# Expert projections of a transformer's last layer: one fp32 product each, or three bf16 products in pairs of experts

## The chip, the cores and the metric

The kernel is one program on one core of a Trainium2 chip. A core has five engines that run their own instruction lists side by side: TensorE (PE in the profile; PEld is its weight load), VectorE (DVE), ScalarE (ACT), GpSimd (POOL) and SyncE (SP), which here only issues DMAs. They meet at semaphores. Matmul results land in PSUM, in eight banks of 128 partitions x 512 fp32 words; GpSimd works on SBUF alone in this kernel. The metric is device microseconds (us) of one execution.

## What is computed

The reference is a stack of four blocks, each a gated cross attention and a gated feed-forward part, on 4 batches x 512 tokens x 128 features. The change is in the last part, a mixture with 16 experts of head dimension 64. Its core:

```python
rw = _gating(hidden_states, sim_matrix, gates)            # (4, 512, 16), softmax over active experts
q = einsum('bte,bted->btd', rw, einsum('btc,ecd->bted', hidden_states, q_proj))
k = einsum('bte,bted->btd', rw, einsum('btc,ecd->bted', hidden_states, k_proj))
v = einsum('bte,bted->btd', rw, einsum('btc,ecd->bted', hidden_states, v_proj))
scores = einsum('bqd,bkd->bqk', q, k) / 8                 # then causal mask
attn = einsum('bqk,bkd->bqd', softmax(scores), v)
mixed = attn[:, :, None, :] * rw[..., None]
return einsum('bted,edc->btc', mixed, o_proj)
```

So q, k and v are each a sum over 16 experts of (token scaled by its expert weight) times the expert's matrix. Everything is fp32 in the reference.

## The kernel before

The kernel runs eight stages one behind the other (numbers 0 to 7 in its names); every engine has one method per stage and its order is the order of the Python code. No scheduler moves anything. The stage that changes is the last, `mixture_*`.

Its order of work is set by `mixture_steps`. Per batch b it yields the steps x = 0 to 15, one per expert, and then the closing step x = 16. Beside the experts of batch b, the steps carry the pieces of attention and output of batch b-1: steps 0 to 5 its softmax attention in four query tiles (`scores`, then `turn` = transpose of the probabilities, then `weigh` = product with v), steps 6 to 14 its output, in 8 pairs of experts (`scale` = spread the pair's weights over partitions, `bring` = product with `o`). After the last batch the pieces of batch 3 run alone.

What one expert needs:
- TensorE, L2464 (`weights_of`): a bf16 selector product that spreads the expert's row of token weights over 128 partitions, in one of four rotating PSUM banks.
- VectorE, L2624: this times the transposed tokens `xt`, written as fp32 to `scaled7`, of which there are four buffers.
- TensorE, `products`, two steps later: L2472, `qk` weights (128 columns) times `scaled7` into bank 4, and L2476, `v` weights (64 columns) into partitions 0 to 63 of bank 5 for even experts and 64 to 127 for odd ones. Both are fp32 with 512 moving columns; the trace shows each such matmul as two records.

At the closing step ScalarE copies bank 4 in two halves (L2547, L2548) and bank 5 (L2551), TensorE adds the two halves of v with four small products (L2489), and VectorE copies the result (L2630). In the attention steps, one tile of scores passes through a chain: TensorE L2498 and the mask L2499, VectorE maximum L2636 and its scaling L2637, ScalarE exponential L2559, VectorE reciprocal L2640 and normalising L2641, TensorE transposes L2504, ScalarE copy L2565, TensorE `weigh` L2512. The output uses TensorE L2464 again (`scale`), VectorE L2648, TensorE L2524 (`bring`).

GpSimd has nothing to do after the router at the start of the stage (L2661, L2662). Splitting fp32 words into a high and a low bf16 half is already done in other stages: `halves` views a word as two bf16 numbers, of which number 1 is the high half of the word, and a subtraction writes (word - high half) over the low half. `products` at L472 then makes three bf16 products (high x high, high x low, low x high). L952 is such a subtraction, on GpSimd, in stage 0, and L708 multiplies its results there with 64-column weights. `onehead_po` is GpSimd's part of stage 2; L415 is the power that every layer normalisation needs.

## Time and profile before

| | us |
|---|---|
| median of 3 runs | 2001.94 (2001.07 to 2005.05) |
| the profiled execution: its own time | 2000.12 |
| the profiled execution: span from first to last instruction | 1998.3 |
| TensorE busy | 1573.0 (79%) |
| VectorE busy | 1167.4 (58%) |
| ScalarE busy | 801.3 (40%) |
| GpSimd busy | 644.1 (32%) |

A busy TensorE is not one at its peak, since its records overlap; how long a matmul holds the engine is read from the distance between starts. The profile also gives the clock that TensorE was granted, as a share of full speed: 1.00 is 2.4 GHz and 0.50 is 1.2 GHz. Times in the trace count from the start of the span.

### The profile page before, as it was taken

The page shows a single profiled execution, that of the slowest core. Times are in us where ns is not written, and L with a number is a line of the kernel's source. Part 1 is how long each engine was busy: PE and PEld are TensorE (multiplying, and loading weights), DVE is VectorE, ACT ScalarE, POOL GpSimd, SP SyncE. Part 2 cuts the span into 40 slices and gives each one's busy share as a digit, 9 for nine tenths or more (in the row PEclk, how much of TensorE's full clock was granted, in tenths as well). Part 3 has the DMA queues.
Part 4 walks back from the last instruction along what each step waited for, and adds up shares of the span by engine and source line. Part 5 has one row for each costly group of instructions (what it writes and reads, how often), then busy time and mean ns, then how long its engine had stood idle before and what let it go on. Part 6 is the DMA issues. An engine that isn't in the chain of part 4 may idle for free.

```text
span 1998.3 us, 31337 instructions
## 1 busy us (share of the span) xinstructions
PE 1573.0 (79%) x11217; PEld 993.7 (50%) x11325; DVE 1167.4 (58%) x2856; ACT 801.3 (40%) x1803; POOL 644.1 (32%) x770
## 2 busy tenths in 40 slices
PE   4899889988998986675268789959957867399997
PEld 2566656666666665553155345524442334224444
DVE  4766676666666654546947656554574566633333
ACT  3666556746655663420034245533213432100011
POOL 3677567756654862500012333000003101100000
PEclk9999989999998997866568799989985788599987
DMA  6223211201111212310000000000000000000000
GB/s 241 67 82 103 71 53 40 52 22 43 48 37 37 55 32 69 103 75 0 0 1 1 10 4 1 2 0 1 1 0 1 1 1 1 0 0 6 6 1 11
DMA packets 35439, 63.89 MB, mean 32 GB/s; under 512 B 7527, under 2 KB 25026, under 8 KB 34131
## 3 DMA queue, kind: packets, MB, share of 16 engines
q1 hardware_dynamic: 33815, 59.77, 10.0%
q0 software_dynamic: 1472, 2.12, 0.3%
q8 instruction: 93, 1.52, 0.3%
q14 instruction: 59, 0.48, 0.1%
HBM read 30.59 MB, written 12.66 MB: 22 GB/s over the span
## 4 chain that ended last, share of the span: by engine, by line
PE 53%; DVE 24%; issue 6%; ACT 5%; DMA 4%; POOL 4%; SPq 2%; ACTq 0%; DVEq 0%; POOLq 0%
PE banks L475 9%; PE banks L693 4%; PE banks L1860 3%; DVE work L738 3%; PE banks L2476 3%; PE banks L682 3%; PE banks L708 3%; PE banks L2472 3%; DVE xn L421 3%; DMA work<-scratch 3%; SPq L987 2%; PE banks L1843 2%; PE banks L634 2%; PE banks L450 2%; PE banks L2524 1%
## 5 line engine op out<-in xcount | busy, mean ns | idle before, releaser
L952 POOL TENSOR_TENSOR work<-work 128x512 bf16<-128x512 f32 (+1 forms) x448 | 373.2, 861 | 59.5 <-ACT work L850 57.6
L835 ACT ACTIVATE work<-banks,work 128x666 f32<-128x666 f32 x256 | 209.1, 817 | 250.5 <-DVE work L738 185.3
L738 DVE TENSOR_REDUCE work<-banks 128x1 f32<-128x666 f32 x256 | 215.8, 843 | 66.8 <-PE banks L682 66.2
L693 PE MATMUL banks<-const,work 128*128 128x128 f32 (+1 forms) x1536 | 229.3, 281 | 22.7 <-ACT work L850 19.3
L415 POOL TENSOR_TENSOR norm_room<-norm_room,minus_half 128x4 f32<-128x4 f32 x48 | 50.1, 1045 | 562.8 <-DVE norm_room L410 562.8
L682 PE MATMUL banks<-work 128*128 128x154 bf16 (+1 forms) x935 | 171.2, 302 | 27.6 <-DMA work<-scratch 21.6
L693 PEld LDWEIGHTS banks<-const,work 128*128 128x128 f32 (+1 forms) x1536 | 156.1, 135 | 54.1 <-issue 20.3
L708 PE MATMUL banks<-work 128*64 128x256 bf16 x2304 | 159.4, 283 | 15.3 <-POOL work L952 14.2
L475 PE MATMUL banks<-work,weights_b 128*128 128x512 bf16 (+1 forms) x830 | 157.2, 347 | 13.2 <-DVE work L2184 5.6
L450 PE MATMUL banks<-const,xn 128*128 128x128 f32 x176 | 40.9, 375 | 142.3 <-DVE xn L421 89.4
L850 ACT ACTIVATE work<-banks 128x512 f32<-128x512 f32 x256 | 151.0, 590 | 3.9 <-PE banks L693 3.8
L682 PEld LDWEIGHTS banks<-work 128*128 128x128 bf16 x1024 | 96.6, 99 | 110.0 <-DMA work<-scratch 28.7
L756 DVE COPY work<-banks 128x256 f32<-128x256 f32 x256 | 106.0, 414 | 63.3 <-PE banks L693 63.1
L708 PEld LDWEIGHTS banks<-work 128*64 128x64 bf16 x2304 | 120.9, 110 | 34.9 <-POOL work L952 17.4
L1937 DVE TENSOR_REDUCE work<-banks 128x2 f32<-128x308 f32 x192 | 86.5, 472 | 83.1 <-PE banks L1815 45.2
L456 ACT ACTIVATE xt<-banks 128x512 f32<-128x512 f32 x48 | 28.5, 597 | 247.4 <-PE banks L450 247.2
L475 PEld LDWEIGHTS banks<-work,weights_b 128*128 128x128 bf16 (+1 forms) x840 | 82.9, 100 | 83.6 <-issue 18.4
L1916 ACT ACTIVATE work<-banks 128x256 f32<-128x256 f32 (+1 forms) x256 | 87.3, 382 | 61.5 <-PE banks L1847 26.9
L450 PEld LDWEIGHTS banks<-const,xn 128*128 128x128 f32 x176 | 26.8, 188 | 154.6 <-DVE xn L421 72.7
L1843 PE MATMUL banks<-work 128*128 128x256 bf16 (+1 forms) x256 | 66.9, 293 | 14.4 <-ACT work L1908 11.6
L750 DVE TENSOR_TENSOR work<-banks,work 128x256 f32<-128x256 f32 x64 | 27.2, 424 | 86.6 <-ACT work L844 86.6
L931 POOL COPY work<-work 128x256 f32<-128x256 f32 x64 | 25.4, 397 | 144.4 <-DVE work L746 144.4
(386 smaller groups left out, 3047.8 us busy)
## 6 DMA issues: line engine op xcount, KB each, us to landing
work<-work SPq DMA_DIRECT2D x128, 166.5 KB, 2.9
sorted<-in_pads SPq DMA_DIRECT2D x10, 838.5 KB
weights_b<-in_weights SPq DMA_DIRECT2D x1, 4120.0 KB, 25.0
work<-scratch SPq DMA_DIRECT2D x64, 64.0 KB, 2.4
weights_b<-in_weights SPq DMA_DIRECT2D x1, 2824.0 KB, 9.8
weights_a<-in_weights SPq DMA_DIRECT2D x1, 2056.0 KB, 8.6
weights_a<-in_weights SPq DMA_DIRECT2D x1, 2050.0 KB, 10.4
work<-work SPq DMA_DIRECT2D x32, 64.0 KB, 1.9
```

Source lines behind the costliest of these rows:

```text
L450: i = pe.transpose(ps[:, j * P:j * P + rows], src[0:rows, j, :], self.eye[0:rows, 0:rows])
L475: m = pe.matmul(out, left(a), right(b), start=start and n == 0, stop=stop and n == 2)
L682: m = pe.matmul(slot[:, a:z], lhs, k[:, h, part, a:z], start=part == 0, stop=part == 1)
L693: m = pe.transpose(ps[0:rows, c:c + P], prob[:, t * P:t * P + rows], self.eye)
L708: m = pe.matmul(self.out_bank[64 * h:64 * h + 64, 0:2 * P], self.v[n % 3][:, t, of_values, 64 * h:64 * h + 64], self.probs_parts[u % 2][:, ...
L738: ve.tensor_reduce(self.neg_max[i % 4], self.slot[i % 2][:, 0:KEYS0], AX_X, ALU.max, negate=True).then_inc(self.mark("max"))
L756: ve.tensor_copy(self.probs_t[u % 2][:, h, 4:KT0, j * P:(j + 1) * P], self.bank_b[:, 0:2 * P].rearrange("p (t n) -> p t n", t=2)).then_inc ...
L835: ac.activation(self.probs[i % 3], self.slot[i % 2][:, 0:KEYS0], ACT.Exp, bias=self.neg_max[i % 4], accum_out=self.sums[u % 2][:, 2 * j + ...
L850: ac.activation(self.probs_t[u % 2][:, h, 0:4, j * P:(j + 1) * P], self.bank_a.rearrange("p (t n) -> p t n", t=4), ACT.Copy).then_inc(self ...
L952: po.tensor_tensor(parts[:, :, :, 0], exact, parts[:, :, :, 1], ALU.subtract).then_inc(self.mark(event, i - 3))
L1843: m = pe.matmul(bank, left, a.q4[b % 2][:, g, cols], start=True, stop=s != 4)
L1916: ac.activation(out, self.bank_of(k, HALF)[0:rows_n, :], ACT.Exp).then_inc(self.mark("exp4", s, n))
```

## The change

Three edits.

1. The fp32 products of `products` become three bf16 products each, made for two experts at a time. The six `qk` products are issued first (L475, from the helper), then six `v` products with even and odd expert alternating. `products` is now called at the odd steps 3, 5, ..., 15 for the pair (x-3, x-2) and at the closing step for the pair (14, 15). Its semaphore counts pairs. `scaled7` has six buffers in place of four.
2. GpSimd makes the low halves of `scaled7`: one subtraction of 128 x 512 per expert and batch, 64 in all, each behind VectorE's multiplication; the products wait for it (`scaled7_low`).
3. GpSimd makes the low halves of the `qk` and `v` weights once, in stage 2: six subtractions of 128 x 512, behind a wait for the weights' DMA.

```diff
     def onehead_po(self, po):
         self.follow_power(po, 1, BATCH - 1)
+        po.wait_ge(*self.at("dma_weights7", 16))
+        for name in ("qk", "v"):
+            for c in range(self.w[7][name].shape[1] // BANK):
+                whole = self.w[7][name][:, c * BANK:(c + 1) * BANK]
+                po.tensor_tensor(self.halves(whole)[:, :, 0], whole, self.halves(whole)[:, :, 1], ALU.subtract).then_inc(self.mark("low7"))
...
-        self.scaled7 = [self.place(SEQ) for _ in range(4)]
+        self.scaled7 = [self.place(SEQ) for _ in range(6)]
...
         def products(b, x):
-            n = E3 * b + x
-            z = self.scaled7[n % 4]
+
+            both = (x, x + 1)
+            words = {e: self.halves(self.scaled7[(E3 * b + e) % 6]) for e in both}
             if x == 0:
                 self.bank(pe, 4, "projected7_k", b)
-            pe.wait_ge(*self.at("scaled7", n))
-            pe.matmul(self.bank_of(4), w["qk"][:, x * P:(x + 1) * P], z, start=x == 0, stop=x == E3 - 1)
-            if x == 0:
                 self.bank(pe, 5, "projected7_v", b)
-            o = slice(64 * (x % 2), 64 * (x % 2) + 64)
-            pe.matmul(self.bank_of(5)[o, :], w["v"][:, x * D3:(x + 1) * D3], z, start=x < 2, stop=x >= E3 - 2).then_inc(self.mark("products7", n))
+            for e in both:
+                pe.wait_ge(*self.at("scaled7_low", E3 * b + e))
+                of = self.halves(w["qk"][:, e * P:(e + 1) * P])
+                self.products(pe, self.bank_of(4), lambda part: of[:, :, 1 - part], lambda part: words[e][:, :, 1 - part], e == 0, e == E3 - 1)
+            for n, (of, at) in enumerate(((1, 1), (1, 0), (0, 1))):
+                for e in both:
+                    o = slice(64 * (e % 2), 64 * (e % 2) + 64)
+                    m = pe.matmul(self.bank_of(5)[o, :], self.halves(w["v"][:, e * D3:(e + 1) * D3])[:, :, of], words[e][:, :, at],
+                                  start=e < 2 and n == 0, stop=e >= E3 - 2 and n == 2)
+            m.then_inc(self.mark("products7", E3 // 2 * b + x // 2))
...
                 weights_of(spread1[0:96, x, :], b, "scaled7", E3 * b + x).then_inc(self.mark("spread_weights7", E3 * b + x))
-                if x >= 2:
-                    products(b, x - 2)
+                if x >= 3 and x % 2:
+                    products(b, x - 3)
             elif x == E3:
                 products(b, E3 - 2)
-                products(b, E3 - 1)
...
                 ve.wait_ge(*self.at("spread_weights7", n))
-                if n >= 4:
-                    ve.wait_ge(*self.at("products7", n - 4))
+                if n >= 6:
+                    ve.wait_ge(*self.at("products7", (n - 6) // 2))
...
         po.memset(self.parts7[0:96, :], 0.0).then_inc(self.mark("clear7"))
+        po.wait_ge(*self.at("clear7", 1))
+        for n in range(BATCH * E3):
+            po.wait_ge(*self.at("scaled7", n))
+            z = self.scaled7[n % 6]
+            po.tensor_tensor(self.halves(z)[:, :, 0], z, self.halves(z)[:, :, 1], ALU.subtract).then_inc(self.mark("scaled7_low", n))
```

Where the instructions stand. First TensorE in batch 0, in the middle of the experts; before, one selector product (L2464) and one expert (L2472, L2476) alternate, with the semaphore that each waits for in brackets:

```order
L2464 MATMUL banks<-work,const_b 128x512 [waits scaled]
L2472 MATMUL banks<-work,weights_a 128x512 [waits scaled]
L2476 MATMUL banks<-work,weights_a 64x512
L2464 MATMUL banks<-work,const_b 128x512 [waits scaled]
L2472 MATMUL banks<-work,weights_a 128x512 [waits scaled]
L2476 MATMUL banks<-work,weights_a 64x512
```

and now (L2470 is the selector, L475 the `qk` products, L2486 the `v` products):

```order
L2470 MATMUL banks<-work,const_b 128x512 [waits scaled] x2
L475 MATMUL banks<-work,weights_a 128x512 [waits scaled_low]
L475 MATMUL banks<-work,weights_a 128x512 x2
L475 MATMUL banks<-work,weights_a 128x512 [waits scaled_low]
L475 MATMUL banks<-work,weights_a 128x512 x2
L2486 MATMUL banks<-work,weights_a 64x512 x6
```

Two selectors now stand together, and a pair's twelve products behind them; the wait of the products is for GpSimd's result in place of VectorE's.

Second, TensorE in a later batch, from step 2 to step 5, where the attention of the batch before runs. Before (L2504 is `turn`, L2498 and L2499 `scores`, L2512 `weigh`):

```order
L2464 MATMUL banks<-work,const_b 128x512
L2472 MATMUL banks<-work,weights_a 128x512
L2476 MATMUL banks<-work,weights_a 64x512
L2504 MATMUL banks<-const,work 128x128 x2
L2498 MATMUL banks<-work 128x256
L2498 MATMUL banks<-work 128x128
L2499 MATMUL banks<-const_b 128x128
L2512 MATMUL banks<-work 128x128
L2464 MATMUL banks<-work,const_b 128x512
L2472 MATMUL banks<-work,weights_a 128x512
L2476 MATMUL banks<-work,weights_a 64x512
L2504 MATMUL banks<-const,work 128x128 x3
```

and now (L2515 is `turn`, L2509 and L2510 `scores`, L2523 `weigh`):

```order
L2470 MATMUL banks<-work,const_b 128x512
L2515 MATMUL banks<-const,work 128x128 x2
L2509 MATMUL banks<-work 128x256
L2509 MATMUL banks<-work 128x128
L2510 MATMUL banks<-const_b 128x128
L2523 MATMUL banks<-work 128x128
L2470 MATMUL banks<-work,const_b 128x512
L475 MATMUL banks<-work,weights_a 128x512 x6
L2486 MATMUL banks<-work,weights_a 64x512 x6
L2515 MATMUL banks<-const,work 128x128 x3
```

The products of step 2 have gone from between the selector and the transposes; those of a pair stand in step 3. Step 4 loses its products in the same way and step 5 has the next pair.

Third, the end of GpSimd's list, which ended with the memset before:

```order
-L2661 TENSOR_TENSOR work<-work,half 128x16
-L2662 MEMSET work 96x2048
-L2726 UNCONDITIONAL_BRANCH
+L2671 TENSOR_TENSOR work<-work,half 128x16
+L2672 MEMSET work 96x2048
+L2677 TENSOR_TENSOR work<-work 128x512 x64
+L2741 UNCONDITIONAL_BRANCH
```

The 64 new subtractions (L2677) run in GpSimd's list behind everything it had.

## Rows read from the trace of the kernel before

In a timeline a row is start (us), length (us), engine, line, operation, operands, count, and in brackets how long the engine had been idle and what ended it.

**Rows 1.** each batch's end at L2547 (start us, us, what, [idle before])
```profile
1785.19 0.59 ACT L2547 ACTIVATE work<-banks 64x512 f32<-64x512 f32 x1 [46.45 <-PE banks L2476]
...
1841.70 0.59 ACT L2547 ACTIVATE work<-banks 64x512 f32<-64x512 f32 x1 [34.24 <-PE banks L2476]
...
1900.05 0.59 ACT L2547 ACTIVATE work<-banks 64x512 f32<-64x512 f32 x1 [34.24 <-PE banks L2476]
...
1959.98 0.59 ACT L2547 ACTIVATE work<-banks 64x512 f32<-64x512 f32 x1 [34.24 <-PE banks L2476]
```

**Rows 2.** critical chain of the stretch 1747 to 1960 us, shares by line
```profile
by line: PE banks L2476 31.0%; PE banks L2472 27.9%; PE banks L2464 11.5%; PE banks L2524 10.3%; PE banks L2498 4.8%; PE banks L2512 3.6%; PE banks L2504 2.8%; PE banks L2489 1.7%; issue 1.4%; DVE work L2624 1.3%; DVE work L2611 1.1%; PE ba
```

**Rows 3.** timeline of the stretch 1756 to 1763 us, one expert of batch 0
```profile
1756.94 0.39 PE L2464 MATMUL banks<-work,const_b 96*128 96x512 bf16 x1
...
1757.17 1.02 PE L2472 MATMUL banks<-work,weights_a 128*128 128x512 f32 x2
...
1757.37 0.69 DVE L2624 TENSOR_TENSOR work<-banks,xt 128x512 f32<-128x512 f32 x1 [1.49 <-PE banks L2464]
...
1758.12 1.07 PE L2476 MATMUL banks<-work,weights_a 128*64 128x512 f32 x2
...
1759.13 0.39 PE L2464 MATMUL banks<-work,const_b 96*128 96x512 bf16 x1
```

**Rows 4.** timeline of ScalarE in stage 5, each start behind 12 bf16 products
```profile
1380.17 0.69 ACT L2174 ACTIVATE work<-banks,weights_b 128x512 f32<-128x512 f32 x1 [1.90 <-PE banks L475]
...
1382.76 0.69 ACT L2174 ACTIVATE work<-banks,weights_b 128x512 f32<-128x512 f32 x1 [1.90 <-PE banks L475]
```

**Rows 5.** timeline of TensorE in stage 1, moving halves of words, 256 columns
```profile
795.70 2.95 PE L475 MATMUL banks<-work,weights_b 128*128 128x256 bf16 x24
...
798.49 0.38 PE L1172 MATMUL banks<-const,work 128*128 128x128 f32 x2
```

**Rows 6.** timeline of TensorE in stage 0, the 64-column products of L708
```profile
401.23 0.73 PE L682 MATMUL banks<-work 128*128 128x512 bf16 x4
...
401.89 1.22 PE L708 MATMUL banks<-work 128*64 128x256 bf16 x18
...
403.04 0.33 PE L693 MATMUL banks<-const,work 128*128 128x128 f32 x1
```

**Rows 7.** instruction groups of GpSimd (xcount | busy us, mean ns | idle before)
```profile
L952 POOL TENSOR_TENSOR work<-work 128x512 bf16<-128x512 f32 x256 | 267.2, 1044 | 59.5 <-ACT work L850 57.6
```

**Rows 8.** timeline of GpSimd in stage 2
```profile
852.63 1.01 POOL L415 TENSOR_TENSOR norm_room<-norm_room,minus_half 128x4 f32<-128x4 f32 x1 [3.68 <-DVE norm_room L410]
...
881.44 1.01 POOL L415 TENSOR_TENSOR norm_room<-norm_room,minus_half 128x4 f32<-128x4 f32 x1 [27.80 <-DVE norm_room L410]
```

**Rows 9.** timeline of batch 1, step 2: scores of tile 1 to their transposes
```profile
1792.02 0.23 PE L2499 MATMUL banks<-const_b 128*128 128x128 bf16 x1
...
1792.83 0.69 DVE L2624 TENSOR_TENSOR work<-banks,xt 128x512 f32<-128x512 f32 x1
...
1793.73 0.35 DVE L2641 TENSOR_SCALAR work<-work 128x256 f32<-128x256 f32 x1
...
1794.27 0.44 PE L2504 MATMUL banks<-const,work 128*128 128x128 f32 x2
```

**Rows 10.** normalising scalings of VectorE, first in stage 0, then behind it
```profile
L421 DVE TENSOR_SCALAR xn<-x,norm_room 128x128 f32<-128x128 f32 x12 | 7.2, 660 | 0.0
...
L421 DVE TENSOR_SCALAR xn<-xn,norm_room 128x128 f32<-128x128 f32 x80 | 23.9, 361 | 5.9 <-POOL norm_room L415 5.6
```

**Rows 11.** timeline of both engines at the router's memset
```profile
1719.51 1.80 POOL L2662 MEMSET work<- 96x2048 bf16 x1
...
1719.60 1.74 DVE L2578 TENSOR_SCALAR work<-work 128x16 f32<-128x16 f32 x1 [5.99 <-POOL work L2661]
```

**Rows 12.** windows: length, busy PE, PEld, DVE, ACT, POOL, then TensorE's clock
```profile
1852.00:1854.00 2.00, 2.00 (x10) 1.05 (x9) 0.00 (x0) 0.38 (x1) 0.00 (x0) 1.00 0.00 0
...
1910.00:1912.00 2.00, 2.00 (x3) 0.29 (x2) 0.01 (x1) 0.00 (x0) 0.00 (x0) 0.50 0.00 0
```

More of the change, by code:

```diff
@@ L2459, in mixture_pe @@
         pe.wait_ge(*self.at("parts7", 1))
+        pe.wait_ge(*self.at("low7", 6))
         self.small_at = {}
@@ L2542, in mixture_ac @@
             if x == E3:
-                n = E3 * b + E3 - 1
-                ac.wait_ge(*self.at("products7", n))
+                ac.wait_ge(*self.at("products7", E3 // 2 * (b + 1) - 1))
                 if b >= 2:
@@ L2621, in mixture_ve @@
                 ve.wait_ge(*self.at("spread_weights7", n))
-                if n >= 4:
-                    ve.wait_ge(*self.at("products7", n - 4))
-                ve.tensor_tensor(self.scaled7[n % 4], self.bank_of(self.small_at["scaled7", n]), self.xt[:, self.cols_of(b)],
+                if n >= 6:
+                    ve.wait_ge(*self.at("products7", (n - 6) // 2))
+                ve.tensor_tensor(self.scaled7[n % 6], self.bank_of(self.small_at["scaled7", n]), self.xt[:, self.cols_of(b)],
                                  ALU.mult).then_inc(self.mark("scaled7", n))
```

## The prediction

> **What bounds the kernel now.** I read the chain of waits of the last stage first: from 1747 to 1960 us it stands almost wholly on TensorE, L2476 (`v`) with 31.0% and L2472 (`qk`) with 27.9%, the selector L2464 with 11.5% [rows 2]. So this stretch of 213 us is a TensorE stretch, and the changed instructions are its largest part. Next the ends of the four batches [rows 1]: the experts of batch 0 end at 1785.2, those of batches 1, 2 and 3 after another 56.5, 58.35 and 59.9 us; the 38 us behind 1960 (attention and output of batch 3) hold no changed product. Then the timeline of one expert of batch 0 [rows 3]: selector to `qk` 0.23 us, `qk` to `v` 0.95, `v` to the next selector 1.01. One expert is 2.18 us, its products 1.95, a pair's 3.9. Last I looked at who else is in the loop: VectorE needs 0.43 us from the selector's start and then 0.69 [rows 3]; GpSimd is idle there.
>
> **TensorE's new price.** Six `qk` products per pair: in stage 5, twelve bf16 products of 128x512 pass in 2.59 us [rows 4], 0.216 each, so 1.30. That the moving side is one half of each fp32 word costs nothing: 24 products of that kind with 256 columns pass in 2.79 us, 0.116 each, a little over half of 0.216 [rows 5]. Six `v` products of 64 columns, even and odd expert in different halves of the array: in stage 0, 18 such products with 256 columns take 1.15 us [rows 6], 0.128 for two, so two run side by side. For 512 columns two together lie between 0.216 (one stream) and 0.256 (twice 0.128); I take 0.235, and 0.70 for three. For entering and leaving the 64-column form I add 0.1: the four L682 products ahead, two with 512 and two with 154 columns, should take 0.56 by the 0.216 and take 0.66 [rows 6]. Sum: 2.1 us per pair, bounds 1.95 and 2.7 (no overlap of the `v` products: 1.30 + 6 x 0.216 + 0.1). Saved 1.8 per pair, 32 pairs: 57.6 us.
>
> The Trainium skill, TensorEngine Tiling (Array Packing), Key Properties, says that a change of tiling mode drains TensorE. The 0.1 above is what the row leaves for it; without any drain the 32 pairs would save 3 us more.
>
> **The new link through GpSimd.** One subtraction of 128x512 takes 1.044 us, mean of 256 of the same form, also in place [rows 7]. Two per pair are 2.1, less than the 2 x 0.23 + 2.1 = 2.56 that a pair of batch 0 takes on TensorE. Latency: from the first selector of a pair 0.43 + 0.69 + 0.1 + 1.04 = 2.3 us until the first low half and 3.3 until the second. Between that selector and the pair's products stand the second selector, the products of the pair ahead and two more selectors: 0.23 + 2.1 + 0.46 = 2.8, and 0.65 more until the odd expert is needed, 3.4. So batch 0 is covered, barely; later batches have the attention or output between and are covered well. In the closing step no selectors stand between, some 0.3 us in each batch. The start of batch 0 waits about a us more than before for the first low halves, but at the half clock it starts with; I leave these small ones against each other.
>
> **Where the products were a cover.** In the attention steps, products hid the softmax chain. In batch 1 the mask of tile 1's scores starts at 1792.02 and VectorE's scaling L2641 runs at 1793.73 for 0.35; the transposes start at 1794.27, just when the 1.95 us of products are over [rows 9]. In the new order steps 2 and 4 have no products; those of a pair stand in steps 3 and 5. So in two steps of each of batches 1 to 3 TensorE waits about 1.9 us: 6 x 1.9 = 11.4 us given back. Steps 3 and 5 stay covered. In the output steps nothing was hidden by products that isn't by `bring` (0.9 us).
>
> **A collision of GpSimd and VectorE.** In stage 0, where GpSimd works much, VectorE's scaling of 128x128 takes 0.66 us on average; later 0.36 [rows 10]. At the router a scaling of 128x16 lasts 1.74 us, from 1719.60 to 1721.34, beside GpSimd's memset from 1719.51 to 1721.31 [rows 11]: it came free with it. L2641 is such a scaling and stands in the softmax chain. Its place is bad: the multiplication L2624 ends at 1793.52, GpSimd would start on the low half at about 1793.6 and end at 1794.65, and L2641, due from 1793.73 to 1794.08, would end near 1794.7 [rows 9, 7, 11]. That is 0.6 us for each of four tiles, 12 tiles: 7.2 us lost; bounds 0 and 12 x 1.04 = 12.5.
>
> The Trainium skill, SBUF — State Buffer, Who interferes with whom, says the same: VectorE's two-port forms (scaling and copy within SBUF) and GpSimd take one port pair in turn, the later one blocks wholly. It also says that an operation with one input in PSUM, as L2624, is not hit; without this rule's effect the sum would be 7 us better.
>
> **The clock.** In batch 2 and 3 TensorE falls to 0.50 of its clock after the wait at the batch's end and the first attention steps, and is back at 1.00 at 1852 in the one case and still at 0.50 at 1910 to 1912 in the other [rows 12]. With the same instructions, batches 2 and 3 are 1.85 and 3.4 us longer than batch 1 [rows 1]: that is the price of a fall, 5.2 in all. The new order has more idle time in just these steps (2.5 us in steps 2 and 4, with the collision). I count a fall as in batch 3 in each batch (3.3), and in every second one another in step 4 (2.2): 3 x 4.4 = 13.2, so 8.0 more than now. Bounds: 5.2 less than now (no fall), and half clock through all attention steps, about 8 per batch.
>
> **GpSimd in stage 2.** Six subtractions are 6.3 us. After its power at 852.63 GpSimd is idle until 881.44 [rows 8], so they are hidden; if the weights' DMA were late, 22 us of slack remain. VectorE could be held for one operation there, 1 us at most; I count nothing.
>
> **Sum.** 57.6 - 11.4 - 7.2 - 8.0 = 31.0 us. The profiled execution had 2000.12 (span 1998.3 and 1.8 around it) and would have 1969.1; the median of the runs is 1.8 above it, so 1971.
>
> **Rivals.**
> A. The chain hides better: the clock falls no more often than now, and L2641 slips in ahead of GpSimd. Then 57.6 - 11.4 = 46 us come through, 1956. For it: batch 1 had two waits of 2 us and no fall; against it: the row at 1793.73, behind GpSimd's start.
> B. The `v` products do not overlap at 512 columns: 0.6 per pair, 32 pairs, 19 us: 1990. For it: no row with this width; against it: the 18 products of stage 0, of the same form [rows 6].
> C. GpSimd becomes the bound of batch 0: if its subtraction with waits takes 1.75 us instead of 1.04, a pair needs 3.5 for 2.56: 8 x 0.95 = 8 us, 1979. Against it: 1.044 over 256 instances with small spread, and output steps of 4.8 us per pair that would hide it anyway.
> D. Slower: TensorE does not get its clock back. All from 1747 to 1960 at 0.50: batch 0 then needs 8 x 5.1 = 41 for 38 us, an output phase of 24.3 us (35.1 now less 6 x 1.8) 48.6, the attention phase about 27 for 18.5, with 3 of boundary 79 per batch: 276 for 213, so 2063. Since a us of work at half clock costs half a us, it decides from about 80 us at half clock beyond today's. Against it: a pair's products are over 4 us of unbroken work at half clock, as ahead of the rises [rows 12], and the output steps leave no gap.
> E. The change doesn't do what it says: the wait on the low halves stalls each pair by the 1.8 it saves. It would need a latency of 5.2 in place of 3.3 in batch 0 and more elsewhere: 2000.
>
> **How the numbers follow.** Forecast 52%, own range 1963 to 1980 (the bounds of collision and clock). A 20%, B 9%, C 11%, D 4%, E 2%, and 2% for anything else slower. The predicted time is the forecast's, 1971. For 8 in 10 the range takes in most of A and C: 1955 to 1984. A measurement can tell 0.2% (4 us) from no change. Faster: forecast, A, B, C and the like, 0.94; slower: D and the else, 0.04; the same: E, 0.02.
>
> **What would show it.** Starts of the closing copy: batch 0 should end near 1770.7 instead of 1785.2, the later batches should take 52 to 53 each (56.5 - 14.4 + 3.8 + 2.4 + 4.4); below 49 speaks for A, above 56 for B or D. The twelve products of a pair should take 2.1 us at full clock (2.7: B). TensorE should idle about 2.5 us before the transposes in steps 2 and 4, ended by L2651, the new number of L2641, and this scaling should last over 0.8 us; if it lasts 0.35 the collision is wrong. GpSimd's subtraction should be 1.04 and never the releaser of a long wait. The sum is wrong if products wait long for `scaled7_low` or if any stage ahead of 1700 us changes by over 2 us.

## The result and the profile after

| | before | after |
|---|---|---|
| median of the runs | 2001.81 (4 runs, 2001.07 to 2005.05) | 1973.09 (4 runs, 1971.97 to 1974.64) |
| span of the profiled execution | 1998.3 | 1971.3 |
| stage 7, start to end | 251.18 | 223.99 |
| TensorE busy | 1573.0 | 1535.3 |
| GpSimd busy | 644.1 | 716.6 |

The ratio is 0.9854, with a 95% interval of 0.9837 to 0.9871. The change makes the kernel 28.7 us faster where 31.0 was predicted; 1973 lies 2 us above the forecast and inside its own range. All of the gain is in stage 7: it starts at 1747.31 us where it started at 1747.12. On the way there the two are not level: GpSimd's power (L415) that runs at 991.70 us in before runs at 994.76 in after, though the two were almost level at 852 (852.63 and 852.37), and the difference is gone again by 1100 us. The prediction had named over 2 us ahead of 1700 as a sign against its sum; the two stretches cancel, and the first 2 us of it stand in e10 below as well, which has no new subtractions.

The stage is counted here from the end of VectorE's last router operation to the end of the span. A batch ends at its first closing copy, as in [rows 1]; in ScalarE's timeline of after:

```profile
1772.11 0.59 ACT L2557 ACTIVATE work<-banks 64x512 f32<-64x512 f32 x1 [33.18 <-PE banks L2486]
1827.08 0.59 ACT L2557 ACTIVATE work<-banks 64x512 f32<-64x512 f32 x1 [24.04 <-PE banks L2486]
1879.26 0.59 ACT L2557 ACTIVATE work<-banks 64x512 f32<-64x512 f32 x1 [24.00 <-PE banks L2486]
1932.97 0.59 ACT L2557 ACTIVATE work<-banks 64x512 f32<-64x512 f32 x1 [24.00 <-PE banks L2486]
```

Against [rows 1]: batch 0 takes 24.80 us (38.07 before), the next three 54.97, 52.18 and 53.71 (56.51, 58.35, 59.93), the tail behind them 38.33 (38.32). The forecast was about 23.5 and 52 to 53. ScalarE's idle time ahead of the copy, which is the output stretch without attention, fell from 34.24 to 24.0 in each later batch. The rest of those batches, the attention part, grew from 22.3, 24.1 and 25.7 us to 30.9, 28.2 and 29.7.

The timeline of one pair in batch 0 gives the new price on TensorE:

```profile
1756.24 0.60 PE L2470 MATMUL banks<-work,const_b 96*128 96x512 bf16 x2
...
1756.69 1.52 PE L475 MATMUL banks<-work,weights_a 128*128 128x512 bf16 x6
...
1758.14 0.87 PE L2486 MATMUL banks<-work,weights_a 128*64 128x512 bf16 x6
...
1758.94 0.60 PE L2470 MATMUL banks<-work,const_b 96*128 96x512 bf16 x2
```

From the first `qk` product to the first `v` product 1.45 us, `v` to the next selector 0.80, together 2.25 (2.1 predicted). The whole pair with its two selectors is 2.70 where two experts were 4.37 (2.19 for one [rows 3]), 1.67 less; batch 0 as a whole, with its start, is shorter by 1.66 for each of its eight pairs.

What was given back stands in TensorE's row of the transposes, over the whole stage (busy us, mean ns, then the idle time ahead and who ended it), in after:

```profile
L2515 PE MATMUL banks<-const,work 128*128 128x128 f32 x40 | 10.2, 369 | 28.5 <-DVE work L2651 28.5
```

and in before, whose line is L2504:

```profile
L2504 PE MATMUL banks<-const,work 128*128 128x128 f32 x40 | 9.4, 340 | 11.5 <-DVE work L2641 11.4
```

Both have the same 40 transposes and the same tail. TensorE waits 17.1 us longer for the normalising scaling; the prediction had 18.6 (11.4 for the lost cover, 7.2 for the collision). One such wait, batch 1 at step 2, in the timeline of all engines of after:

```profile
1780.55 0.69 DVE L2634 TENSOR_TENSOR work<-banks,xt 128x512 f32<-128x512 f32 x1
...
1781.26 0.16 DVE L2650 RECIPROCAL work<-work 128x1 f32<-128x1 f32 x1
1781.32 1.04 POOL L2677 TENSOR_TENSOR work<-work 128x512 bf16<-128x512 f32 x1 [2.67 <-DVE work L2634]
1781.46 1.05 DVE L2651 TENSOR_SCALAR work<-work 128x256 f32<-128x256 f32 x1
...
1782.66 0.66 PE L2515 MATMUL banks<-const,work 128*128 128x128 f32 x2 [2.46 <-DVE work L2651]
```

GpSimd starts 0.14 us before the scaling, and the scaling ends at 1782.51, 0.15 us behind GpSimd's end: 1.05 us for what took 0.35 in [rows 9]. In step 3 the scaling is as long, but there the pair's products stand between it and the transposes, and TensorE does not wait; in the timeline of all engines of after:

```profile
1786.91 1.23 DVE L2651 TENSOR_SCALAR work<-work 128x384 f32<-128x384 f32 x1
...
1789.99 0.72 PE L2515 MATMUL banks<-const,work 128*128 128x128 f32 x3
```

The multiplication L2634, with an input in PSUM, is not held up. At the start of batch 0 four of them pass in 2.48 us, most of it under GpSimd's subtractions; the mean of all 64 is 688 ns, and it is the same 688 in e2 below, where GpSimd does nothing:

```profile
1748.01 2.48 DVE L2634 TENSOR_TENSOR work<-banks,xt 128x512 f32<-128x512 f32 x4 [0.70 <-PE banks L2470]
...
1748.84 4.04 POOL L2677 TENSOR_TENSOR work<-work 128x512 bf16<-128x512 f32 x4 [27.34 <-DVE work L2634]
```

GpSimd itself is no bound. Its groups, in after: 64 subtractions of 1043 ns, and in the whole stage the products wait 0.8 us for it, all at the start of batch 0.

```profile
L2677 POOL TENSOR_TENSOR work<-work 128x512 bf16<-128x512 f32 x64 | 66.2, 1043 | 143.4 <-DVE work L2634 143.3
...
L475 PE MATMUL banks<-work,weights_a 128*128 128x512 bf16 x192 | 56.1, 433 | 0.8 <-POOL work L2677 0.8
```

The six of stage 2 lie in the gap of [rows 8], in GpSimd's timeline of after:

```profile
853.34 6.03 POOL L1436 TENSOR_TENSOR weights_a<-weights_a 128x512 bf16<-128x512 f32 x6
883.18 1.01 POOL L415 TENSOR_TENSOR norm_room<-norm_room,minus_half 128x4 f32<-128x4 f32 x1 [23.81 <-DVE norm_room L410]
```

The clock, in windows of after (length, busy times of the five engines, then the granted clock):

```profile
1784.00:1786.00 2.00, 2.00 (x9) 1.34 (x8) 0.71 (x2) 0.07 (x1) 0.00 (x0) 0.50 0.03 8
...
1836.00:1838.00 2.00, 0.33 (x2) 0.29 (x2) 1.47 (x3) 0.24 (x2) 1.04 (x1) 0.50 0.01 4
...
1892.00:1894.00 2.00, 2.00 (x8) 1.24 (x8) 0.72 (x3) 0.20 (x1) 0.00 (x0) 0.50 0.00 0
1904.00:1906.00 2.00, 2.00 (x6) 0.58 (x4) 0.59 (x1) 0.00 (x0) 1.04 (x1) 0.50 0.00 0
```

In each of batches 1 to 3 TensorE is at 0.50 behind the first attention waits. In batches 1 and 3 it comes back and falls once more at step 4's wait (0.50 at 1794 to 1796 and at 1904 to 1906), in batch 2 it does not, and batch 2 is the shortest. In before batch 1 kept 1.00 throughout, and batches 2 and 3 had one fall each.

### The profile page after: what moved, and what is told of

Its sections match the earlier page's. It is cut to its first block, busy times and chain, and to the rows that moved or that the text cites. A ratio compares the mean times of both kernels' runs of the same rounds, so it can differ in the third digit from the quotient of the medians.

```text
span 1971.3 us, 31770 instructions
## 1 busy us (share of the span) xinstructions
PE 1535.3 (78%) x11453; PEld 989.6 (50%) x11453; DVE 1174.9 (60%) x2856; ACT 801.4 (41%) x1803; POOL 716.6 (36%) x840
## 4 chain that ended last, share of the span: by engine, by line
PE 52%; DVE 26%; issue 6%; ACT 5%; POOL 4%; DMA 4%; SPq 2%; ACTq 0%; DVEq 0%; POOLq 0%
PE banks L475 12%; PE banks L693 4%; PE banks L682 4%; PE banks L1865 4%; DVE work L738 3%; PE banks L708 3%; DMA work<-scratch 3%; DVE xn L421 3%; SPq L987 2%; PE banks L1848 2%; PE banks L634 2%; PE banks L450 2%; PE banks L2535 1%; PE banks L1774 1%; DVE norm_room L405 1%
## 5 line engine op out<-in xcount | busy, mean ns | idle before, releaser
L415 POOL TENSOR_TENSOR norm_room<-norm_room,minus_half 128x4 f32<-128x4 f32 x48 | 50.2, 1045 | 558.8 <-DVE norm_room L410 558.8
L682 PE MATMUL banks<-work 128*128 128x512 bf16 (+1 forms) x1024 | 191.6, 310 | 21.1 <-DMA work<-scratch 21.1
L708 PE MATMUL banks<-work 128*64 128x256 bf16 x2304 | 158.8, 282 | 14.5 <-POOL work L952 13.3
L475 PE MATMUL banks<-work,weights_b 128*128 128x512 bf16 (+1 forms) x840 | 159.3, 349 | 11.5 <-DVE work L2189 5.2
L708 PEld LDWEIGHTS banks<-work 128*64 128x64 bf16 x2304 | 120.5, 110 | 34.2 <-POOL work L952 16.7
L475 PEld LDWEIGHTS banks<-work,weights_b 128*128 128x128 bf16 (+1 forms) x840 | 83.2, 100 | 83.4 <-issue 18.0
L2677 POOL TENSOR_TENSOR work<-work 128x512 bf16<-128x512 f32 x64 | 66.2, 1043 | 143.4 <-DVE work L2634 143.3
L750 DVE TENSOR_TENSOR work<-banks,work 128x256 f32<-128x256 f32 x64 | 27.2, 425 | 87.0 <-ACT work L844 87.0
```

What stands on the lines that cost most here:

```text
L475: m = pe.matmul(out, left(a), right(b), start=start and n == 0, stop=stop and n == 2)
L682: m = pe.matmul(slot[:, a:z], lhs, k[:, h, part, a:z], start=part == 0, stop=part == 1)
L708: m = pe.matmul(self.out_bank[64 * h:64 * h + 64, 0:2 * P], self.v[n % 3][:, t, of_values, 64 * h:64 * h + 64], self.probs_parts[u % 2][:, ...
```

## The experiments

The theory: the products are 1.66 us per pair cheaper; the attention steps give back 17 us by lost cover and by the collision; the rest is lost to the granted clock. The rivals: the gap to the forecast lies in the `v` products (their order, or their form), in the price of reading halves of words, or in another stage.

Stage 7 of every kernel, as above, in us of the profiled executions:

| kernel | batch 0 | 1 | 2 | 3 | tail | stage |
|---|---|---|---|---|---|---|
| before | 38.07 | 56.51 | 58.35 | 59.93 | 38.32 | 251.18 |
| after | 24.80 | 54.97 | 52.18 | 53.71 | 38.33 | 223.99 |
| e1_low_after_scaling | 25.78 | 52.38 | 49.47 | 50.76 | 38.37 | 216.76 |
| e2_no_subtraction | 23.75 | 49.39 | 50.77 | 50.79 | 38.30 | 213.00 |
| e3_v_one_after_other | 24.86 | 52.28 | 53.78 | 52.16 | 38.40 | 221.48 |
| e4_v_128_columns | 23.30 | 52.00 | 51.01 | 54.33 | 40.97 | 221.61 |
| e6_busy_in_waits | 24.78 | 48.85 | 48.85 | 48.86 | 33.26 | 204.60 |
| e7_late_low_and_cover | 24.80 | 46.42 | 51.21 | 51.19 | 40.98 | 214.60 |
| e8_late_cover_busy | 24.80 | 44.60 | 44.60 | 44.60 | 33.34 | 191.94 |
| e9_contiguous_tokens | 25.13 | 53.09 | 51.61 | 51.53 | 38.32 | 219.68 |
| e10_before_busy | 38.09 | 56.38 | 56.38 | 56.38 | 33.33 | 240.56 |
| e11_v_same_half | 30.20 | 58.94 | 57.95 | 58.00 | 37.72 | 242.81 |

The unchanged stages ahead end between 1745 and 1757 us in these kernels, so a whole time carries up to 12 us that the edit did not make; where few us matter I go by the stage.

**e1_low_after_scaling.** In the attention steps GpSimd's subtraction waits until the step's scaling is done.

```diff
             po.wait_ge(*self.at("scaled7", n))
+            if n >= E3 and 1 <= n % E3 <= QT:
+                po.wait_ge(*self.at("weights7", QT * (n // E3 - 1) + n % E3 - 1))
```

> The changed kernel (1973.1 us) with one wait more: in steps 1 to 4 of batches 1 to 3, GpSimd's subtraction waits until VectorE's scaling of the probabilities (L2651) is through. Theory (the collision costs time): L2651 goes back from 0.85-1.03 us to 0.3-0.5, TensorE's wait before the transposes shrinks by 0.3 to 0.8 in steps 1, 2 and 4, about 2 us per batch, so 1965 to 1968. Rival (the long L2651 is covered, or the wait is set by ScalarE): 1972 to 1974, with GpSimd merely later. The wait could also make the low halves late for the products of step 3 or 5; then a wait of L475 on GpSimd shows.

Measured: 1967.49 us (1965.93 to 1970.94), 0.9817 of before (0.9798 to 0.9836); stage 216.76, 7.2 less than after: batches 1 to 3 are 8.25 shorter, and batch 0, whose instructions did not change, is 1.0 longer, at half clock until about 1756. VectorE's groups from 1745 to 1940 us, in after:

```profile
L2651 DVE TENSOR_SCALAR work<-work 128x384 f32<-128x384 f32 x3 | 3.7, 1229 | 0.1
L2651 DVE TENSOR_SCALAR work<-work 128x128 f32<-128x128 f32 x4 | 3.6, 893 | 0.1
...
L2651 DVE TENSOR_SCALAR work<-work 128x256 f32<-128x256 f32 x3 | 3.2, 1053 | 0.1
...
L2651 DVE TENSOR_SCALAR work<-work 128x512 f32<-128x512 f32 x3 | 2.9, 973 | 0.1
```

and in this kernel:

```profile
L2651 DVE TENSOR_SCALAR work<-work 128x512 f32<-128x512 f32 x3 | 1.5, 486 | 0.1
L2651 DVE TENSOR_SCALAR work<-work 128x256 f32<-128x256 f32 x4 | 1.4, 353 | 0.1
L2651 DVE TENSOR_SCALAR work<-work 128x384 f32<-128x384 f32 x3 | 1.3, 420 | 0.1
L2651 DVE TENSOR_SCALAR work<-work 128x128 f32<-128x128 f32 x4 | 1.1, 286 | 0.1
```

The window holds one scaling of 128x128 of the tail, which nothing disturbs; without it the three others of after are 1095 ns. Against e1 the twelve are longer by 0.81, 0.70, 0.81 and 0.49 us, times three: 8.4 us, 0.70 each. So the collision is shown, by undoing it; the forecast had 0.6. TensorE's waits before the transposes fell by 6.6 us, from 28.5 to 21.9:

```profile
L2515 PE MATMUL banks<-const,work 128*128 128x128 f32 x40 | 9.8, 352 | 21.9 <-DVE work L2651 21.9
```

The collision is waited for only in steps 1, 2 and 4; the 0.81 of step 3, 2.4 in all, lie under the products. That leaves 6.0 of the 6.6; the rest is that step 1's undisturbed wait is 1.86 us at full and 1.27 at half clock, and after has two of its three at full clock where e1 has one. What is left of the 17.1 us of new waits when nothing collides is the lost cover: 21.9 - 11.4 = 10.5 us in six waits of 1.55 to 1.88, 1.75 on average.

The Trainium skill, SBUF — State Buffer, Who interferes with whom, names this pair: a scaling within SBUF can take VectorE's two-port form, which shares a port pair with GpSimd, and the one that issues first keeps it for its whole instruction. These rows agree: GpSimd began 0.14 us earlier, and the scaling ended 0.15 us behind it. It also leaves out an operation like L2634, with one input in PSUM and one in SBUF, and that one stays at 0.69.

**e2_no_subtraction.** The 64 subtractions are left out, and the products that read the low half of the scaled tokens read the high half.

```diff
-                pe.wait_ge(*self.at("scaled7_low", E3 * b + e))
+                pe.wait_ge(*self.at("scaled7", E3 * b + e))
...
-                self.products(pe, self.bank_of(4), lambda part: of[:, :, 1 - part], lambda part: words[e][:, :, 1 - part], e == 0, e == E3 - 1)
+                self.products(pe, self.bank_of(4), lambda part: of[:, :, 1 - part], lambda part: words[e][:, :, 1], e == 0, e == E3 - 1)
...
-                    m = pe.matmul(self.bank_of(5)[o, :], self.halves(w["v"][:, e * D3:(e + 1) * D3])[:, :, of], words[e][:, :, at],
+                    m = pe.matmul(self.bank_of(5)[o, :], self.halves(w["v"][:, e * D3:(e + 1) * D3])[:, :, of], words[e][:, :, 1],
...
-            po.wait_ge(*self.at("scaled7", n))
-            z = self.scaled7[n % 6]
-            po.tensor_tensor(self.halves(z)[:, :, 0], z, self.halves(z)[:, :, 1], ALU.subtract).then_inc(self.mark("scaled7_low", n))
```

> The changed kernel without GpSimd's 64 subtractions: the products read the high half of the scaled tokens in place of the low half, so q, k and v lack the low part of the tokens; number and form of the products are the same, and they wait for VectorE. Theory (GpSimd costs time only through the collision, and about 1 us at the start of batch 0): 1964 to 1967, within 2 us of the run that moves the subtractions behind the scaling. Rival (the latency of the low halves holds the products too): 4 us or more below that run, and batch 0 shorter than 24.7 us by more than 1.5.

Measured: 1964.72 us (1963.97 to 1967.72), 0.9805 (0.9787 to 0.9823); stage 213.00, 11.0 below after and 3.8 below e1. TensorE's waits before the transposes are 22.0 us, as in e1. So taking GpSimd's work away altogether brings, against e1, 2.0 in batch 0 (23.75 against 25.78) and 1.7 in the later batches and the tail. Of the 2.0, 1.0 is what e1's batch 0 is longer than after's (24.80) with the same instructions; the other 1.05 is the link through GpSimd at the start, where after has a wait of 0.8. The 1.7 cannot be a wait, since the waits are e1's; it goes with the clock, which in e1 falls a second time in batch 1 (0.54 at 1798 to 1800) and here in no batch. GpSimd's work costs nothing more that is large.

**e3_v_one_after_other.** The three `v` products of the even expert first, then the three of the odd one, instead of alternating.

```diff
-            for n, (of, at) in enumerate(((1, 1), (1, 0), (0, 1))):
-                for e in both:
+            for e in both:
+                for n, (of, at) in enumerate(((1, 1), (1, 0), (0, 1))):
```

> The changed kernel with the six v products of a pair in another order: three of the even expert, then three of the odd one. Theory (even and odd products run side by side only when they alternate): six times 0.216 instead of 0.65 us, 0.65 more per pair, 32 pairs: 1992 to 1995. Rival (they do not overlap in either order, and the 0.80 us from the first v product to the next selector comes from something else, or they overlap in any order): 1972 to 1975.

Measured: 1975.16 us (1971.89 to 1975.64), 0.9852 (0.9835 to 0.9870). The pair has not changed, in TensorE's timeline of this kernel:

```profile
1758.00 1.52 PE L475 MATMUL banks<-work,weights_a 128*128 128x512 bf16 x6
1759.46 0.88 PE L2486 MATMUL banks<-work,weights_a 128*64 128x512 bf16 x6
1760.27 0.60 PE L2470 MATMUL banks<-work,const_b 96*128 96x512 bf16 x2
1760.71 1.52 PE L475 MATMUL banks<-work,weights_a 128*128 128x512 bf16 x6
```

0.81 for `v`, 2.71 for the pair. That the alternation is what lets two products run side by side is refuted. The stage is 2.5 us shorter than after's: batches 1 and 3 are shorter by 2.7 and 1.6 and batch 2 is longer by 1.6, and it is batch 2 that has the second fall of the clock here (0.50 at 1850 to 1852), where in after it was 1 and 3.

**e11_v_same_half.** To see whether there is any overlap, both experts of a pair write to the same half of bank 5 (pairs 0, 2, 4, 6 the lower, the others the upper), so that each half holds other experts' sums. The two halves are added after the last pair, so `v` itself stays what it was, unlike what the expectation says.

```diff
-                    o = slice(64 * (e % 2), 64 * (e % 2) + 64)
+                    o = slice(64 * (e // 2 % 2), 64 * (e // 2 % 2) + 64)
...
-                                  start=e < 2 and n == 0, stop=e >= E3 - 2 and n == 2)
+                                  start=e in (0, 2) and n == 0, stop=e in (E3 - 3, E3 - 1) and n == 2)
```

> The changed kernel with both experts of a pair in the same half of the array for v, 0 to 63 for one pair and 64 to 127 for the next, so the sums of v are not the reference's; number, form and order of the products are the same. Six v products take 0.80 us now, in either order. Theory (even and odd expert overlap because they use different halves): about 1.4 us instead of 0.80, pair of batch 0 3.3 instead of 2.70, stage 19 us longer, 243. Rival (a 64-column product is short by itself): 0.80 and 224.

Measured, a single run: 1991.72 us, stage 242.81. TensorE's timeline of this kernel:

```profile
1761.19 1.52 PE L475 MATMUL banks<-work,weights_a 128*128 128x512 bf16 x6
1762.64 1.54 PE L2486 MATMUL banks<-work,weights_a 128*64 128x512 bf16 x6
1764.12 0.60 PE L2470 MATMUL banks<-work,const_b 96*128 96x512 bf16 x2
1764.56 1.52 PE L475 MATMUL banks<-work,weights_a 128*128 128x512 bf16 x6
```

The six now take 1.48 us, 0.25 each, and the pair 3.37. So the overlap is real and worth 0.68 us per pair, 21.8 in all, with 18.8 seen in the stage. It hangs on the two halves (64 columns of the array each, with their 64 partitions of the bank), not on the order; which of the two, array or bank, this run cannot separate. The forecast's rival B (no overlap, 19 us) had its price right and did not happen.

**e4_v_128_columns.** The `v` products as three of 128 columns on the even expert's tokens; the odd expert's `v` is left out. No 64-column product remains among the experts.

```diff
-                for e in both:
-                    o = slice(64 * (e % 2), 64 * (e % 2) + 64)
-                    m = pe.matmul(self.bank_of(5)[o, :], self.halves(w["v"][:, e * D3:(e + 1) * D3])[:, :, of], words[e][:, :, at],
-                                  start=e < 2 and n == 0, stop=e >= E3 - 2 and n == 2)
+                m = pe.matmul(self.bank_of(5), self.halves(w["v"][:, x * D3:(x + 2) * D3])[:, :, of], words[x][:, :, at],
+                              start=x == 0 and n == 0, stop=x == E3 - 2 and n == 2)
```

> The changed kernel with the v products of a pair as three products of 128 columns that multiply the even expert's tokens with both experts' weights; the odd expert's v is left out, and no 64-column product stands in the loop. A pair takes 2.25 us now (1.45 and 0.80). Theory (0.3 us of it is the change between the 128-column and 64-column forms, 0.15 each way): nine products of 0.216, 1.95 us, 0.3 less per pair, 32 pairs, at most 9.6: 1963 to 1966. Rival (the 0.3 us are in the wait for the second low half or the loads of halves): 1972 to 1974.

Measured: 1978.17 us (1969.19 to 1981.06), 0.9856 (0.9830 to 0.9882); by the whole time nothing, where 1963 to 1966 was expected. The stage starts 7.5 us later than in after, in code that is the same, its tail is 2.6 longer, at 0.50 until about 1964, and in each of batches 1 to 3 the clock falls at least twice; so of 32 x 0.22 = 7.0 us the stage shows only 2.4. The pair shows the edit, in TensorE's timeline of this kernel:

```profile
1761.28 1.52 PE L475 MATMUL banks<-work,weights_a 128*128 128x512 bf16 x6
1762.65 0.84 PE L2484 MATMUL banks<-work,weights_a 128*128 128x512 bf16 x3
1763.33 0.59 PE L2470 MATMUL banks<-work,const_b 96*128 96x512 bf16 x2
1763.76 1.52 PE L475 MATMUL banks<-work,weights_a 128*128 128x512 bf16 x6
```

`qk` 1.37, `v` 0.68, the pair 2.48: 0.22 less than in after, of which 0.12 lies in `v`, 0.08 in `qk` and 0.02 at the selectors. The Trainium skill, TensorEngine Tiling (Array Packing), Key Properties, has it that a change of tiling mode drains TensorE; the 0.22 are what the 64-column form costs here for entering, leaving and its own six products, and 0.3 was expected. The forecast had 0.16 for the same: the 0.1 read from [rows 6], and 0.06 by which 3 x 0.235 is more than 3 x 0.216. How much of the 0.22 is a drain is not separated.

**e9_contiguous_tokens.** All products read the first 512 bf16 numbers of the buffer in a row instead of one half of each of its 512 words, so they multiply other numbers; the count, the sizes and the weights' side are the same.

```diff
+            plain = {e: self.scaled7[(E3 * b + e) % 6].bitcast(BF16)[:, 0:SEQ] for e in both}
...
-                self.products(pe, self.bank_of(4), lambda part: of[:, :, 1 - part], lambda part: words[e][:, :, 1 - part], e == 0, e == E3 - 1)
+                self.products(pe, self.bank_of(4), lambda part: of[:, :, 1 - part], lambda part: plain[e], e == 0, e == E3 - 1)
...
-                    m = pe.matmul(self.bank_of(5)[o, :], self.halves(w["v"][:, e * D3:(e + 1) * D3])[:, :, of], words[e][:, :, at],
+                    m = pe.matmul(self.bank_of(5)[o, :], self.halves(w["v"][:, e * D3:(e + 1) * D3])[:, :, of], plain[e],
```

> The changed kernel with the moving side of all new products read as 512 neighbouring bf16 numbers in place of one half of each of 512 words; they multiply other numbers, so q, k and v are not the reference's; counts, weights, waits and GpSimd's work are the same. Six qk products take 1.45 us now up to the first v product, 0.15 more than 6 x 0.216. Theory (reading halves of words costs: 24 products with 256 such columns took 0.116 each, twice that is 0.232): 0.12 to 0.15 us less per pair, pair of batch 0 2.56 to 2.58 instead of 2.70, stage 4 us shorter, 219 to 221. Rival (the reading is free and the 0.15 is at the change of form): 2.69 to 2.71 and stage 223 to 225.

Measured: 1967.84 us (1966.62 to 1970.36), 0.9833 (0.9805 to 0.9860); stage 219.68, 4.3 below after. TensorE's timeline of this kernel:

```profile
1755.35 1.46 PE L475 MATMUL banks<-work,weights_a 128*128 128x512 bf16 x6
1756.74 0.84 PE L2487 MATMUL banks<-work,weights_a 128*64 128x512 bf16 x6
1757.51 0.61 PE L2470 MATMUL banks<-work,const_b 96*128 96x512 bf16 x2
1757.95 1.46 PE L475 MATMUL banks<-work,weights_a 128*128 128x512 bf16 x6
```

`qk` 1.39, `v` 0.77, pair 2.60: reading every second bf16 number costs 0.10 per pair, 3.2 us in 32, and two thirds of the 0.15 that the products term was short.

**e6_busy_in_waits.** After, with eight unneeded selector products in each wait that the clock fell behind: at the batch's end and before the transposes of steps 1, 2 and 4, and before all four of the tail. They write to a bank that is overwritten next.

```diff
+        def busy(bank, n):
+            for _ in range(n):
+                pe.matmul(bank, spread1[0:96, 0, :], self.parts7[0:96, 0:BANK], start=True, stop=True)
...
+                busy(bank, 8)
                 pe.wait_ge(*self.at("projected7_v", b))
...
+                    if t != 2 or o == BATCH - 1:
+                        busy(bank, 8)
                     pe.wait_ge(*self.at("weights7", tile))
```

> The changed kernel (last stage 224.0 us from the first selector to the end, tail behind the last products 38.3) with eight unneeded bf16 products, 1.7 us at full clock, in each wait of TensorE: at the closing copies, ahead of the transposes of steps 1, 2 and 4, and in the tail. They go into a bank that is overwritten next. Theory (the waits cost a second time, by the clock: about 4.4 us per batch, and the tail from 1937 to 1958 us runs at half clock): granted clock 1.00 through the stage, batches 1 to 3 near 49 us instead of 53.6, the tail 5 us shorter, stage 204 to 210. Rival (the half clock falls on latency that would be there anyway, or the added products delay what follows): stage 222 to 230.

Measured: 1958.21 us (1950.83 to 1963.35), 0.9770 (0.9741 to 0.9799); stage 204.60, 19.4 below after, though its stage starts 9.6 us later. The three later batches are all 48.85. Ten us of the tail, from 7 us behind its start on, as windows, in after:

```profile
1940.00:1950.00 10.00, 6.27 (x19) 3.97 (x19) 2.39 (x8) 2.11 (x6) 0.00 (x0) 0.50 0.00 0
```

and in this kernel, where the tail starts 4.7 us earlier:

```profile
1935.00:1945.00 10.00, 9.37 (x50) 5.12 (x48) 3.50 (x12) 2.89 (x8) 0.00 (x0) 1.00 0.00 0
```

So the clock cost after 14.3 us in batches 1 to 3 (4.8 each, forecast 4.4) and 5.1 in the tail.

**e10_before_busy.** The same with the kernel before (no unneeded products at steps 2 and 4, whose waits its own products cover).

```diff
+        def busy(bank, n):
+            for _ in range(n):
+                pe.matmul(bank, spread1[0:96, 0, :], self.parts7[0:96, 0:BANK], start=True, stop=True)
...
+                busy(bank, 8)
                 pe.wait_ge(*self.at("projected7_v", b))
...
+                    if t == 0 or o == BATCH - 1:
+                        busy(bank, 8)
                     pe.wait_ge(*self.at("weights7", tile))
```

> The kernel before (stage 251.2 us; batches 38.1, 56.5, 58.35, 59.9; tail 38.3) with eight unneeded bf16 products in its waits: closing copies, ahead of the transposes of step 1, and in the tail. Theory (batches 2 and 3 were longer than batch 1 by the clock alone, and the changed kernel lost 4.8 per batch to it, so that the change without the clock is worth 251.2 - 10.2 less 204.6, some 36 us): batches 1 to 3 all 56.5 to 56.7, tail 33.3, stage 240 to 242. Rival (batch 1 was long for another reason or batches 2 and 3 are): they stay unequal, stage over 245.

Measured: 1989.93 us (1986.05 to 1990.71), 0.9945 (0.9932 to 0.9957); stage 240.56, with 56.38 in each later batch and a tail of 33.33. The clock in windows of this kernel over experts and attention of all batches:

```profile
1745.00:1960.00 215.00, 212.02 (x780) 91.10 (x780) 82.02 (x158) 22.06 (x53) 0.00 (x0) 0.98 0.02 4
```

The clock cost before 10.6 us: 5.65 in the batches (forecast 5.2) and 5.0 in the tail. With e6, the change is worth 240.56 - 204.60 = 36.0 us where the clock holds and 27.2 where it does not: 8.8 us went to the clock, forecast 8.0. These 36.0 are what is left of 53 on the products after the 17.1 of waits.

This run also tells something of the stages ahead, where its instructions are before's. GpSimd's power follows the one ahead of it by 28.81 us in before (852.63 to 881.44), by 30.81 in after and by 30.82 here, without any subtraction in stage 2: the 16 matmuls L1318 in between start at 873.1 in all three and take 4.04 us in before and 5.83 in the other two, where the clock has fallen by 872 to 874 us (0.55 and 0.59 in after and here, 1.00 in before). So the 2 us that after loses there are the clock's and not the subtractions'.

**e7_late_low_and_cover.** e1, and the first two pairs of batches 1 to 3 at steps 2 and 4 instead of 3 and 5 (the other pairs at 7, 9, ..., 15), so that they lie in the waits.

```diff
-                if x >= 3 and x % 2:
-                    products(b, x - 3)
+                at = {2: 0, 4: 2, 7: 4, 9: 6, 11: 8, 13: 10, 15: 12} if b else {i: i - 3 for i in range(3, E3, 2)}
+                if x in at:
+                    products(b, at[x])
```

> The run with GpSimd behind the scaling (stage 216.8 us, batches 52.4, 49.5, 50.8), and in batches 1 to 3 the first two pairs' products in steps 2 and 4 instead of 3 and 5, where they cover the softmax chain of tiles 1 and 3; tile 2 in step 3 is then the only one uncovered. Theory (each uncovered chain costs 1.9 us): one wait instead of two per batch, 5.7 us less, more if the clock falls less: stage 208 to 212. Rival (the clock decides, and one gap is as good as two at letting it fall): 214 to 218. Waits of step 5 for the copied probabilities, which have been under products, could take 0.3 to 0.8 back.

Measured: 1967.83 us (1966.43 to 1971.57), 0.9827 (0.9800 to 0.9855), no different from e1; stage 214.60. Batch 1 has 46.42, but batches 2 and 3 have 51.2, no better than in e1, and the tail 40.98. The windows of this kernel show why (the first is of batch 1, the second of batch 2):

```profile
1780.00:1790.00 10.00, 6.18 (x35) 3.42 (x36) 4.33 (x12) 3.24 (x9) 3.04 (x3) 1.00 0.00 0
...
1826.00:1836.00 10.00, 6.73 (x27) 3.70 (x24) 3.86 (x10) 3.04 (x8) 2.09 (x2) 0.65 0.00 0
```

In batches 2 and 3 the clock falls behind the wait at the batch's end (0.74 at 1828 to 1830, and 0.50 from there on), and at half clock the covers come at twice their length; in batch 1 the same waits were followed by no fall until step 3. Since step 3 is bare in this order, the new place can cover one of two chains: TensorE's waits before the transposes of batches 1 to 3 fell from 14.9 us in e1 to 9.8. Of these 5.1 us the stage shows 2.2: batch 0 is 1.0 shorter and batch 1 6.0, but batches 2 and 3 are 2.2 longer together and the tail 2.6. The expected 208 to 212 did not come, the rival's 214 to 218 did.

**e8_late_cover_busy.** e7 with unneeded products in what waits it leaves: eight at the batch's end, seven before the transposes of steps 1 and 3 and of the tail.

```diff
+                busy(bank, 8)
                 pe.wait_ge(*self.at("projected7_v", b))
...
+                    if t in (0, 2) or o == BATCH - 1:
+                        busy(bank, 7)
                     pe.wait_ge(*self.at("weights7", tile))
```

> All three: GpSimd behind the scaling, products in steps 2 and 4, and unneeded products in the waits that are left (closing copies, steps 1 and 3, tail). If the three costs add up (collision, uncovered chains, clock): batches 1 to 3 near 43.3 + 1.9 + 0.5 = 46 us, tail 33, stage 24.5 + 138 + 33 = 195 to 200, and the run 1946 to 1952. If they overlap: stage 203 to 208.

Measured: 1948.43 us (1943.72 to 1948.84), 0.9723 (0.9695 to 0.9750); stage 191.94. The whole time is as expected, the stage below the expected 195 to 200. It beats both kernels: its stage is 59 us below before's and 32 below after's, the latter from three small edits. TensorE's transposes wait 2.6 us in the whole stage:

```profile
L2523 PE MATMUL banks<-const,work 128*128 128x128 f32 x40 | 7.9, 295 | 2.7 <-DVE work L2659 2.6
```

That its later batches are 4.25 shorter than e6's gives the worth of the new cover and of the undisturbed scaling together when the clock holds: 12.75 us, where the change had added 17.1 of waits.

## Why the prediction was right

By its own steps, with spans (27.0 us measured):

- **TensorE's price.** Forecast 2.1 us for a pair's products, saved 57.6. Measured 2.25, and 1.66 saved per pair (batch 0 alone, 38.07 to 24.80, is 1.66 x 8), x 32 = 53.1. This is the term that was mis-sized, by 4.5 us. Two readings were too kind. From 0.116 for 256 columns [rows 5] I concluded that halves of words cost nothing; twice 0.116 is 0.232, 7% over the 0.216 of [rows 4], and e9 finds 0.10 per pair for it. And the 64-column form costs 0.22 (e4) where the sum held 0.16.
- **Lost covers and collision.** 11.4 + 7.2 = 18.6 forecast, 17.1 measured in one row. e1 divides them: lost cover 10.5, 1.75 for each of six chains where I had 1.9, and collision 6.6. The collision's sum came out better than its working. I had 0.6 for each of twelve tiles; the scalings are 0.70 longer on average, but three of the twelve are covered by products, which the forecast counted as waits.
- **The clock.** 8.0 forecast, 8.8 measured (e6 against e10), and the mechanism is shown by taking the fall away on both sides. The pattern was forecast too: one fall in each batch, a second one at step 4 in every second batch. How often the second fall comes was a guess, though: in e3, whose attention steps are the same, it came in batch 2 alone.
- **GpSimd's link.** Latency as forecast: in batch 0 the two low halves are done 2.2 and 3.2 us behind the first selector (forecast 2.3 and 3.3); 0.8 us of waiting in the stage, at its start. C did not happen. Stage 2's subtractions are hidden (e10).
- **Sum.** 53.1 - 17.1 - 8.8 = 27.2, the stage's 27.2, to the few tenths that the reading of a pair leaves open (1.67 in the middle of batch 0 would give 53.4). The spans differ by 27.0, since the stage starts 0.2 us later. Against the forecast's 31.0 the products fell short by 4.5 and the clock by 0.8, and the waits were 1.5 better, so a small part of the miss cancelled.

The stated chances have a slip: D with 4% and the 2% for anything else slower make 0.06 for slower, not 0.04. Of the rivals, A (no collision, no more falls) names what e1 and e6 had to make by hand. D's mechanism, work at half clock behind the waits, was there, but cost only 8.8 us more than it did before; the unbroken output stretch gave the clock back each time.

What stays open: how the 0.22 of e4 divide between a drain and the products themselves; why the clock falls in one batch and not in another with the same waits; and why unchanged stages ahead end up to 12 us apart from one kernel to the next. At the one place compared under e10, 2 us come from where the clock falls; the rest was not traced.

## What to carry to other kernels

Three bf16 products for one fp32 product pay only as far as TensorE stays the bound: count what the old, slower products were hiding, and put the new ones where the waits are. Price the helper engine twice, for its own time and for whom it blocks: here 1.04 us of work on an otherwise idle GpSimd cost VectorE 0.70 in the chain that TensorE waited for, and a wait of one line in GpSimd's list gave it back. Before leaving a wait on TensorE, look at the granted clock behind it: unneeded products in the waits were worth 19.4 us in the changed kernel (e6) and 10.6 in the old one (e10), where the change itself was worth 27.2.

## What the runs showed that I had not expected

- The tail runs at 0.50 for some 20 us in every version without unneeded products (before from 1964 to 1985 us, after from 1937 to 1957): 38.3 us of it become 33.3 with them (e6, e8, e10). I had counted it as untouched.
- Two 64-column products in different halves of the array run side by side whatever the order in which they are issued, also three of the one half ahead of three of the other: 0.81 against 0.80 us (e3), but 1.48 in the same half (e11).
- Reading every second bf16 number makes a moving operand of 512 about 0.01 us slower, `qk` 1.45 against 1.39 for six (e9).
- Cover alone did not keep the clock up: e7's batches 2 and 3 took 51.2, no less than e1's 49.5 and 50.8, and 44.60 in e8, where the waits left were filled too.
